# Scores of two softmax layers taken in row groups of 32 and 64 partitions, with the causal mask ahead of the score

## The chip, the cores and the metric

One core of a Trainium2 chip runs the whole program. The metric is the device time of one execution in microseconds (us). The engines are PE (TensorE, matrix products; PEld is its weight load), DVE (VectorE), ACT (ScalarE), POOL (GpSimd) and SP (SyncE, which issues most DMAs).

## What is computed

Four layers on x of 4 x 512 tokens x 128, each of the form x + attention(norm(x)) + ffn(norm(x)). The change touches the attention of layers 1 and 2:

```python
# layer 1: 16 heads of 8, each split in halves of 4: 32 causal softmax problems per batch
a1 = causal(q1, k1, v1); a2 = causal(q2, k2, v2)     # s = q k' * scale; mask; softmax; p v
y  = concat(a1 - lp * a2, a1 + lp * a2) @ Wo.T
# layer 2: 16 heads of 8, no mask
attn = softmax(Q K' / sqrt(8)); out = attn V
```

Layer 0 has windowed attention and a mixture of experts, layer 1 a second mixture of experts, layer 3 a linear attention and a dense feed-forward part.

## The kernel before

Each engine runs a fixed list of instructions. Steps of ten streams (norms, attention, feed-forward and so on) are merged into one order by the string `MERGE`: each letter takes the next step of its stream, and every engine runs its part of each step in that order. Engines meet through semaphores, and an engine that waits holds up all that stands behind on it.

For each batch b of layer 1 and 2, `stack` (L2007 to L2041, SP) stores q and k, each split in three bfloat16 parts, to DRAM and loads them back side by side, so that one bfloat16 matmul over 96 rows gives a float32 product. The rows of one head (24 in layer 1, 48 in layer 2) are spread over the 96, and those of other heads meet zeros in k. A few rows more (12 or 6) carry minus the row maximum against ones in k, which are loaded from a constant, `kone`; layer 2's k is cleared by POOL first (L1906).

Then two sweeps over the scores follow. **Maxima**: `mx` makes a unit of up to 512 columns in one of two banks of PSUM (ring `topb`), and DVE reduces it (L1485). Layer 1 has 88 such units a batch: a head's row tile sees 512, 384, 256 or 128 keys, and units of 256 or 128 are put together to 512; layer 2 has 64. **Exponentials**: `ex` makes the transposed score of one head and one key tile in one of two other banks (ring `scoreb`), with the maximum subtracted by the extra rows, and ACT takes the exponential into `pbuf` (L1820): 128 a batch in layer 1 (512, 384, 256 and 128 columns), 64 in layer 2 (512). In layer 1 a mask matmul of 128 columns over 128 rows (`identb` and `mdiagT`) is added behind each score. **Products**: `pv` multiplies four tiles of exponentials with v in float32, into four column strips of one bank, so that it uses the shape of 128 rows x 32 columns. It stands in the stream of `ex`, behind the second `ex` of the next step. `mx` of batch b+1 runs beside `ex` of batch b, with the experts of layer 1 between.

The touched lines of `mx` on PE are:

```python
m = mm(bank[:, o:o + k], HQ[lay][i][0:96, h % 8, t * P:(t + 1) * P], HK[lay][i][0:96, kof(lay, h), 0:k], True, not CAUSAL[lay])
if CAUSAL[lay]:
    m = mm(bank[:, o + k - P:o + k], mdiagT, identb, False, True)
```

Of the kernel before, what the change touches and what calls it, by code (L numbers as in the profile page):

```python
# [26 lines left out]
MERGE = (
    "11ab2ab7c2b2c2bc2bcbcbc3bcb4cb4cb3cb2cbc2b2c2bcbcj4cj2cb2c2jb2j4c3j4cbjcjc2jbjc2j2cb2cjcj2cj8c3j5cjc"
    "2j2cb2j2cj2cb2jcjc3jbc2j2bjb5j9b2cb5cbc3b3c2b3cbcb6cb2cjcjbj4cj3c2jb3c2jbcd2jcj5c2jb3j3cjb2j3c2j2cj2"
    "cb2j2cjc2jb2j3cj3cjcj2b3jb2jc2jcjcjcb4cj2c3bcbc5bcb4cb3c2b3c3b2c3bj3cb2c2jbc2jcjc2jb5jb5jb4jcb2ja4jb"  # L30
    "ja4ja2jb2j2b2jdjdjbj15bd3bdbcjbjadjba4jdjb3ja2jb4jc2jb3jd2cb2ja2jc3jba4ja7jc2j2d2eaed2ea3ea2ec79e2cd"
    "2cdc4bd5bdbd2bd7b2d3bcdbcbc6b3e2bebebeb2e2bebebe2bebebebebe3b2eb2e2bedb2e2bebe2bebebebcebe2cebe2cebe"
    "2bce2becbc3bdc2bc2e4bc2b3cb2ece2b2ebebe2becbebebcebcecec3bcdc2e2c5bcbebc2bece2bec2b2eb2cebebebecb2e2"
    "c2ebe2bebebcebebebcb2ecbc2e3c2b2ecebcbecdce2bebebebecb2e2bcebc2bc2ebcbcbcbebebd2b2e2be2bebcebebecece"
    "b2cb2c2ed2e3b2ecebce2cec2be2bebe2bebebcebe2ce2bce2cebe2bebe3c2edcbcdbc2e2cebcecbc2bdebcebc2b2c2bec2b"
    "ebce2bcebe2bebeb2ebcebecece4cbe3bdbceb2c2becbc2ecbecbceb2ecb2eb3c2e3b2ebebe3b2ecedcbecb2e2ce2c2eb2ce"
    "2becbeb2e2bec3be2bc2bcebceb2cece5bebebe3bebeb2cb2eb2cb2ce2bec2b3cbe3bec3b2e2cbcb2e3cec4b2e4bebebcbeb"
    "cbe3cbec2b2c3bcbecec5bcbcbe3b2cbebe2becb3c6bcbc4bc3bcbecbec3bcbc2be5bce5bebe4bcb2ebcbc2ecbe2bebe2b2e"
    "4be2be4b2e4be3bebe8bce2ba3b2ea5be4ba2bebe3be2be4b2e4be2bebe2be7bc5bab2e2beba2bebe3be6b2e5be4be6be2be"
    "5be9bcbebe3be7bc2bc2b2e8be3be10ba6bd2bdbd6bd4bd2bcd3bd4bc8b2ebaebebe2be2be2bebe4b2e3baebe3be4ba2e5b2"  # L40
    "e4bebe2bebe2bebebe2bebe2bebebe2bebe3bebe3bebdbe5be6bebe3bedbe2bebe2bebebe3bebed2be3b2e3bebe2bebe2beb"
    "e2bebe2bebecbebc2bebe6be2b2e8b2e3be2bebe2b2e2beb2ebdbde3bd4bed4babedbeaebe3ba2e3b2e2bedebe3bd5bebe8b"
    "ebebebebebebebe2bebebe2b2e2bebe2b2e2b2eb2e2bebebebebe2bebe2bebebcebe2bebebebebe2be2bcb2eb2e2bedebaeb"
    "eb2e2bebe2bea2e5ba2e3bebe2b2e2bebe2bebe2be2bece2be3be2b2eb2e2bebebebebe2bebe2be2b2e2b2e2b2e2bebeb2e2"
    "bebebebebe2bebe2bebebe2b2e3bebe4beb2eb2eb2e2bebe2b2e2bebebebcebe4b2ebab2e2bebece2bebebeaebecbe4be2be"
    "4baebe2b2e2bebebebebe2bebe3bebebebe2b2e2bebebebe2b2e2bebe2bebe2be2b2e2b2e2be2bc4bd2b2cbg3bf2bgcg4bf2"
    "bagbg3bg3bg2bcfba3bfbf2bg4bf3bfbgc2bf4bf3bg3bf2bg3bfg4bfbc2bc3bf4bfbc5babg5bc4bcbgbhbfc2hbfb2hahaghc"
    "ahih4c2ig2c2i4cihihcicih2cih2cich2cichchcici2cici6c")
# [107 lines left out]
def build(nc, d, out):  # L156
    ctx = ExitStack()
    with ctx:
# [122 lines left out]
        def kof(lay, h):  # L281
            return h % 8 // 4 * 4 + h // 8 if lay == 1 else h

        def tile_of(lay, n):
# [3 lines left out]
            return [(4 * n + j, 4 * n + j) for j in range(4)]

        def tops_of(lay):  # L290
            if lay == 2:
                return [((g, t, 0),) for g in range(16) for t in range(4)]
            todo = []
            for g in range(0, 32, 4):
                todo += [((g + j, t, 0),) for t in (3, 2) for j in range(4)]
                todo += [((g + j, 1, 0), (g + j + 1, 1, 2 * P)) for j in (0, 2)]
                todo.append(tuple((g + j, 0, j * P) for j in range(4)))
            return todo
# [2071 lines left out]
```

## Time and profile before

| | us |
|---|---|
| median of 3 runs (1527.28 to 1532.28) | 1531.0 |
| the profiled execution | 1529.98 |
| its span, first to last instruction | 1528.2 |
| first maxima of layer 1 alone | 588 to 676 |
| exponentials of layer 1, with maxima and experts | 676 to 1201 |
| exponentials of layer 2, with maxima | 1201 to 1447 |

The stages are read from the first and last instructions of L1485 and L1820 for each batch. A float32 matmul is recorded as two instructions. A matmul's recorded duration is its latency; what it takes of PE is the distance of its start from the next one's.

### The profile page before, as it was taken

The numbers are of one execution on the slowest core, as the hardware profiler recorded it, in microseconds if no ns is written. First come the engines' busy times: TensorE is split into PE (matmuls) and PEld (weight loads), VectorE is DVE, ScalarE is ACT, GpSimd is POOL, SyncE is SP. The second block draws the span as 40 slices with busy tenths as digits, with TensorE's granted clock in tenths as the row PEclk, the third lists the DMA queues.
The fourth block names the chain that finished last, engine by engine and source line by source line (L and its number), as shares of the span: only waits on it lengthen the run. The fifth ranks groups of instructions, "written<-read, shape, count | busy, mean of one in ns | idle before, by whom it ended". The sixth has DMA issues, their size and how long they took to land.

```text
span 1528.2 us, 23814 instructions
## 1 busy us (share of the span) xinstructions
PE 1342.3 (88%) x9318; PEld 812.0 (53%) x9334; DVE 970.2 (63%) x2093; ACT 665.5 (44%) x1424; POOL 203.0 (13%) x189
## 2 busy tenths in 40 slices
PE   7977788998897787888989989999779899999999
PEld 4455657876765674343756656654334323234565
DVE  3568743343453677876877876465667888876365
ACT  2444143753541431023433435666446566666621
POOL 1132170000202300035000000044100100000000
PEclk8988698998996987569999999999989999999988
DMA  8000123341000310015253363211212303000000
GB/s 248 6 1 1 29 67 100 98 113 49 27 1 14 70 22 3 0 41 146 89 130 109 107 168 120 92 45 29 64 20 53 64 5 66 3 1 28 1 8 21
DMA packets 65100, 86.22 MB, mean 56 GB/s; under 512 B 9566, under 2 KB 49374, under 8 KB 63326
## 3 DMA queue, kind: packets, MB, share of 16 engines
q1 hardware_dynamic: 60892, 76.30, 19.1%
q0 software_dynamic: 4096, 8.40, 2.0%
q8 instruction: 74, 1.21, 0.3%
q14 instruction: 38, 0.31, 0.1%
HBM read 62.19 MB, written 22.48 MB: 55 GB/s over the span
## 4 chain that ended last, share of the span: by engine, by line
PE 64%; DVE 14%; DMA 8%; ACT 4%; issue 4%; POOL 3%; SPq 2%; DVEq 0%; ACTq 0%
PE psA L404 32%; PE psB L404 25%; PE psB L408 5%; DVE mx L1485 3%; POOL slots_x L1922 2%; PE psA L408 2%; ACT pbuf L1738 2%; DMA wA<-slots_x 2%; POOL tH L1935 1%; DVE st L1168 1%; ACT pbuf L1820 1%; DMA arena<-scr1k 1%; DMA scr1k<-arena 1%; DMA arena<-slots_x 1%; DMA arena<-scr2k 1%
## 5 line engine op out<-in xcount | busy, mean ns | idle before, releaser
L1820 ACT ACTIVATE pbuf<-psA 128x512 f32<-128x512 f32 (+3 forms) x768 | 350.0, 489 | 250.2 <-PE psA L404 243.1
L1485 DVE TENSOR_REDUCE mx<-psA 128x1 f32<-128x512 f32 (+3 forms) x608 | 377.7, 657 | 101.2 <-PE psA L404 97.2
L404 PE MATMUL psA<-arena 64*64 64x128 f32 (+9 forms) x1632 | 243.2, 308 | 14.0 <-DVE mx L1485 11.1
L404 PEld LDWEIGHTS psA<-arena 64*64 64x64 f32 (+3 forms) x1632 | 131.5, 138 | 115.2 <-DVE mx L1485 44.2
L1738 ACT ACTIVATE pbuf<-psA,st,rq 128x128 f32<-128x128 f32 x256 | 92.7, 467 | 112.8 <-DVE st L1172 112.8
L404 PE MATMUL psA<-arena,w 96*128 96x512 bf16 (+4 forms) x320 | 114.8, 411 | 19.3 <-DMA arena<-scr2k 10.4
L404 PE MATMUL psA<-w_identb,w_mdiagT 128*128 128x128 bf16 x512 | 110.9, 243 | 0.0
L404 PE MATMUL psA<-w_mdiagT,w_identb 128*128 128x128 bf16 x512 | 110.0, 223 | 0.0
L404 PE MATMUL psB<-xf,wA 128*128 128x128 f32 x624 | 93.8, 295 | 6.1 <-DMA wA<-in_moe 5.7
L404 PE MATMUL psB<-pbuf,arena 128*5 128x512 f32 (+3 forms) x1024 | 95.3, 445 | 0.4 <-ACT pbuf L1820 0.4
L1935 POOL DMA_INDIRECT tH<-slots_y,slot_i x64 | 62.0, 968 | 237.7 <-DMA slots_y<-tH 219.3
L404 PEld LDWEIGHTS psB<-xf,wA 128*128 128x128 f32 x624 | 82.1, 204 | 13.9 <-issue 10.2
L1879 POOL TENSOR_TENSOR sm<-sm,w_ohalf 128x4 f32<-128x4 f32 x24 | 24.3, 1032 | 461.2 <-DVE sm L1045 461.0
L404 PE MATMUL psA<-w,arena 102*128 102x512 bf16 (+5 forms) x272 | 82.2, 340 | 2.2 <-ACT pbuf L1820 1.7
L1168 DVE TENSOR_REDUCE st<-psA 128x8 f32<-128x1024 f32 x32 | 39.1, 1221 | 71.0 <-PE psA L404 71.0
L1922 POOL DMA_INDIRECT slots_x<-tH,slot_i x64 | 62.1, 970 | 131.5 <-DVE slot_i L1319 74.6
L404 PEld LDWEIGHTS psA<-arena,w 96*128 96x128 bf16 (+1 forms) x320 | 38.2, 122 | 71.2 <-DVE mx L1485 27.1
L404 PE MATMUL psA<-arena,wide 128*64 128x8 f32 (+4 forms) x320 | 64.9, 301 | 11.0 <-DMA arena<-scr1k 8.1
L404 PE MATMUL psA<-arena,pbuf 128*128 128x65 f32 x512 | 70.6, 284 | 2.7 <-DVE pbuf L1192 2.6
L404 PEld LDWEIGHTS psA<-arena,pbuf 128*128 128x128 f32 x512 | 67.4, 204 | 8.8 <-issue 4.5
L404 PE MATMUL psB<-pbuf,res 128*9 128x512 f32 x512 | 66.9, 595 | 1.5 <-ACT pbuf L1820 1.4
L408 PE MATMUL psA<-w_ident,pbuf 128*128 128x128 f32 x272 | 45.3, 292 | 19.1 <-ACT pbuf L1738 10.7
(295 smaller groups left out, 2136.2 us busy)
## 6 DMA issues: line engine op xcount, KB each, us to landing
wA<-in_moe SPq DMA_DIRECT2D x39, 576.0 KB, 3.8
wA<-in_moe SPq DMA_DIRECT2D x39, 256.0 KB, 3.0
slots_x<-wA SPq DMA_DIRECT2D x20, 256.0 KB, 3.7
slots_y<-tH SPq DMA_DIRECT2D x18, 256.0 KB, 3.6
wA<-slots_x SPq DMA_DIRECT2D x15, 256.0 KB, 4.1
arena<-scr2k SPq DMA_DIRECT2D x48, 64.0 KB
scr1q<-arena SPq DMA_DIRECT2D x4, 384.0 KB, 4.0
scr1k<-arena SPq DMA_DIRECT2D x4, 384.0 KB, 4.1
```

The costliest lines, as they stand in the source:

```text
L404: return pe.matmul(out, lhsT, rhs, start=start, stop=stop, skip_group_check=True)
L408: return pe.transpose(out, in_, ident[0:n, 0:n])
L1168: dv.tensor_reduce(mx_, both("S", b, i).rearrange("p x (k c) -> p x k c", k=4), AX.X, ALU.max).then_inc(*s_max.up(b, i))
L1485: dv.tensor_reduce(m[:, t, h:h + c], topb("mx", lay, b, n)[:, 0:c * k].rearrange("p (c k) -> p c k", c=c), AX.X, ALU.max) \
L1738: a = ac.activation(sm[:, k, :], S[:, x, P * k:P * k + P], ACT.Exp, bias=st[:, 8 + 4 * x + k:9 + 4 * x + k], scale=rq(b)[:, 4 * h + k, kv, ...
L1820: ac.activation(pb(lay, b, s, j)[:, 0:T - q0_], scoreb("ex", lay, b, s, j)[:, 0:T - q0_], ACT.Exp, bias=0.0, scale=1.0) \
L1879: po.tensor_tensor(st[:, 4:8], st[:, 0:4], W["ohalf"][:, 0:4], ALU.pow).then_inc(*ln_pow.up(tag, b))
L1922: po.indirect_dma_start(Xs[lay], IndirectOffsetOnAxis(i, 0), tok[:, t * P:(t + 1) * P], None) \
L1935: po.indirect_dma_start(tH(*u)[:, t * P:(t + 1) * P], None, Ys[lay], IndirectOffsetOnAxis(i, 0)) \
```

## The change

- A head's own rows only. A score matmul now takes 24 rows (27 with the maximum) that begin at partition 0, 32, 64 or 96 in layer 1, and 48 (51) that begin at 0 or 64 in layer 2. PE is used by these in shapes of 32 x 128 and 64 x 128 instead of 128 x 128. The lists of units are reordered so that one unit and the next of a sweep use different row groups. Masks keep their 128 rows.
- The mask is written first, and the score is added to it. In `mx` one mask matmul serves all tiles of a unit: 352 in place of 512; in `ex` it stays 512.
- `stack` loads each row group by itself: 48 DMAs in place of 9 for a batch of layer 1, 24 in place of 18 in layer 2; the maxima come in 4 or 2 DMAs in place of 1. Layer 1's k takes a quarter of the bytes. `kone` is gone: POOL sets all of k to one (three memsets of 128 x 512 for layer 1 and three of 128 x 2048 in place of 128 x 4096 for layer 2).
- Buffers of k are smaller, so batch 0 of layer 2 waits for products of layer 1's batch 1 and no longer of batch 2; the ring of exponentials has 12 tiles in place of 8.
- `pv`, `tail` and the projection become an eleventh stream `k`, and `MERGE` is a new string for the whole program.

```diff
-        pb = Ring(ptiles)
+        pb = Ring(ptiles + [arena[:, 7680 + T * k:8192 + T * k] for k in range(4)])
...
+        HS = {1: 32, 2: 64}
+        HO = {1: (0, 1, 2, 3), 2: (0, 2, 1, 3)}
...
+        def q_of(lay, i, h, rows):
+            p = HS[lay] * (h // 8)
+            return HQ[lay][i][p:p + 6 * HD[lay] + rows, h % 8, :]
+
+        def k_of(lay, i, h, rows):
+            p = HS[lay] * (h // 8)
+            return HK[lay][i][p:p + 6 * HD[lay] + rows, h % 8 // 4 if lay == 1 else h % 8, :]
...
-                return [((g, t, 0),) for g in range(16) for t in range(4)]
+                return [((8 * u + g, t, 0),) for g in range(8) for t in range(4) for u in range(2)]
...
+                todo += [tuple((8 * j + g, t, o) for g, t, o in u) for u in units for j in range(4)]
...
-                i, bank = b % NBUF, topb(*u)
-                for h, t, o in tops_of(lay)[n]:
-                    k = (t + 1) * P if CAUSAL[lay] else T
-                    m = mm(bank[:, o:o + k], HQ[lay][i][0:96, h % 8, t * P:(t + 1) * P], HK[lay][i][0:96, kof(lay, h), 0:k],
-                           True, not CAUSAL[lay])
-                    if CAUSAL[lay]:
-                        m = mm(bank[:, o + k - P:o + k], mdiagT, identb, False, True)
+                i, bank, part = b % NBUF, topb(*u), tops_of(lay)[n]
+                t, c = part[0][1], len(part)
+                k = (t + 1) * P if CAUSAL[lay] else T
+                if CAUSAL[lay]:
+                    mm(bank[:, 0:c * k].rearrange("p (c k) -> p c k", c=c)[:, :, k - P:k], mdiagT,
+                       identb.unsqueeze(1).to_broadcast([P, c, P]), True, False)
+                for h, t, o in part:
+                    m = mm(bank[:, o:o + k], q_of(lay, i, h, 0)[:, t * P:(t + 1) * P], k_of(lay, i, h, 0)[:, 0:k], not CAUSAL[lay], True)
...
-                m = mm(bank[:, 0:T - q0_], HK[lay][i][0:HR[lay], kof(lay, g), kb * P:(kb + 1) * P],
-                       HQ[lay][i][0:HR[lay], g % 8, q0_:T], True, not causal)
                 if causal:
-                    m = mm(bank[:, 0:P], identb, mdiagT, False, True)
-                m.then_inc(*ex_mm.up(lay, b, s, j))
+                    mm(bank[:, 0:P], identb, mdiagT, True, False)
+                mm(bank[:, 0:T - q0_], k_of(lay, i, g, 3)[:, kb * P:(kb + 1) * P], q_of(lay, i, g, 3)[:, q0_:T], not causal, True) \
+                    .then_inc(*ex_mm.up(lay, b, s, j))
...
+                for j in range(P // HS[lay]):
+                    r, rows = HS[lay] * j, slice(HS[lay] * j, HS[lay] * j + HS[lay])
+                    for part, n in ((0, 3), (1, 2), (2, 1)):
+                        qs = dr["q"][b][part, rows].rearrange("(i g) c -> i g c", g=8)
                         for k in range(n):
...
+                            sy.dma_start(HQ[lay][i][r:r + D], qs).then_inc(*stack_in[b].up(lay))
+                            ks = dr["k"][b][k, rows].rearrange("(i g) c -> i g c", g=8)
```

**PE in layer 1**, where scores of `ex` (`psA<-w,arena`) and of `mx` (`psA<-arena,wide`) stand in a row with masks (`w_identb`, `w_mdiagT`). Before:

```order
1706 L404 MATMUL psA<-w,arena 128x256
1707 L404 MATMUL psA<-w_mdiagT,w_identb 128x128
1708 L404 MATMUL psA<-arena,wide 128x256
1709 L404 MATMUL psA<-w_identb,w_mdiagT 128x128
1710 L404 MATMUL psA<-arena,wide 128x256
1711 L404 MATMUL psA<-w_identb,w_mdiagT 128x128
```

After:

```order
1502 L412 MATMUL psA<-w_identb,w_mdiagT 128x512
1503 L412 MATMUL psA<-arena,wide 128x128 x4
1504 L412 MATMUL psA<-w_mdiagT,w_identb 128x128
1505 L412 MATMUL psA<-w,arena 128x256
1506 L412 MATMUL psA<-w_identb,w_mdiagT 128x512
1507 L412 MATMUL psA<-arena,wide 128x128 x4
```

The mask has moved ahead of its score, and one of 512 columns stands for four; between the scores of two units there is still a mask. All rows of before take 96 to 128 rows of PE; of after the masks take 128 and the scores 24 or 27.

**PE in layer 2**, where `psA<-wide,arena` and `psA<-arena,wA` are scores of `ex` and of `mx`, and `psB<-pbuf,res` is `pv`. Before:

```order
3060 L404 MATMUL psB<-pbuf,res 9x512 x4
3061 L404 MATMUL psA<-arena,wA 128x512
3062 L404 MATMUL psA<-wide,arena 128x512
3063 L404 MATMUL psA<-arena,wA 128x512
3064 L404 MATMUL psA<-wide,arena 128x512 x2
3065 L404 MATMUL psA<-arena,wA 128x512 x2
3066 L404 MATMUL psA<-wide,arena 128x512
3067 L404 MATMUL psB<-pbuf,res 9x512 x4
```

After:

```order
2764 L412 MATMUL psB<-pbuf,res 9x512 x4
2765 L412 MATMUL psA<-arena,wA 128x512
2766 L412 MATMUL psA<-wide,arena 128x512 x2
2767 L412 MATMUL psA<-arena,wA 128x512
2768 L412 MATMUL psA<-wide,arena 128x512
2769 L412 MATMUL psA<-arena,wA 128x512
2770 L412 MATMUL psA<-wide,arena 128x512 x2
2771 L412 MATMUL psA<-arena,wA 128x512 x2
2772 L412 MATMUL psB<-pbuf,res 9x512 x4
```

Scores stand side by side here as before, now with rows 0 to 50 for one and 64 to 114 for the other, and more or fewer than eight of them may stand between two `pv`.

**SP**, the loads of one batch of layer 1 behind the two stores. Before, all of them:

```order
227 L2030 DMA w<-scr1q 16x4096 x3
228 L2033 DMA arena<-scr1k 48x4096
229 L2030 DMA w<-scr1q 16x4096 x2
230 L2033 DMA arena<-scr1k 32x4096
231 L2030 DMA w<-scr1q 16x4096
232 L2033 DMA arena<-scr1k 16x4096
```

After, the first of 24 such pairs:

```order
267 L2025 DMA w<-scr1q 4x4096
268 L2029 DMA arena<-scr1k 4x2x512
269 L2025 DMA w<-scr1q 4x4096
270 L2029 DMA arena<-scr1k 4x2x512
271 L2025 DMA w<-scr1q 4x4096
```

Nine DMAs of 16 to 48 rows became 48 of 4 rows.

## Rows read from the trace of the kernel before

**Rows 1.** The page, section 1 (busy us, share) and the clock of section 2
```profile
PE 1342.3 (88%) x9318; PEld 812.0 (53%) x9334; DVE 970.2 (63%) x2093; ACT 665.5 (44%) x1424; POOL 203.0 (13%) x189
PEclk8988698998996987569999999999989999999988
```
**Rows 2.** Busy time by stretch: stretch and length, busy by engine, granted clock, DMA share, GB/s
```profile
588.00:676.00 88.00, 71.82 (x342) 34.82 (x343) 71.23 (x155) 3.78 (x8) 8.99 (x9) 0.55 0.02 7
676.00:843.00 167.00, 147.73 (x1269) 95.90 (x1268) 122.92 (x246) 68.85 (x163) 30.72 (x31) 0.94 0.44 117
843.00:1000.00 157.00, 144.00 (x1318) 102.53 (x1316) 105.71 (x215) 71.18 (x169) 0.78 (x1) 0.98 0.41 119
1000.00:1117.00 117.00, 97.01 (x827) 46.74 (x825) 66.07 (x136) 65.87 (x162) 38.84 (x36) 0.94 0.21 47
1117.00:1201.00 84.00, 79.55 (x595) 35.11 (x594) 68.54 (x138) 48.55 (x119) 4.55 (x2) 0.97 0.15 27
1201.00:1447.00 246.00, 236.08 (x1313) 88.66 (x1311) 183.44 (x371) 155.41 (x287) 4.03 (x4) 1.00 0.12 25
```
**Rows 3.** Groups by form: name, count, busy us, mean ns, idle before
```profile
L404 PE MATMUL psA<-w_identb,w_mdiagT 128*128 128x128 bf16 x512 | 110.9, 243 | 0.0
L1820 ACT ACTIVATE pbuf<-psA 128x512 f32<-128x512 f32 x384 | 213.2, 596 | 89.6 <-PE psA L404 87.3
L1485 DVE TENSOR_REDUCE mx<-psA 128x1 f32<-128x512 f32 x384 | 248.2, 685 | 63.6 <-PE psA L404 62.4
L404 PE MATMUL psA<-arena 64*64 64x128 f32 x1024 | 69.5, 291 | 0.0
```
**Rows 4.** PE in order of time, layer 1: start, us, name, rows*columns used
```profile
691.46 0.38 PE L404 MATMUL psA<-arena 108*128 108x512 bf16 x1
691.68 0.22 PE L404 MATMUL psA<-w_mdiagT,w_identb 128*128 128x128 bf16 x1
691.74 0.38 PE L404 MATMUL psA<-arena 108*128 108x512 bf16 x1
691.96 0.22 PE L404 MATMUL psA<-w_mdiagT,w_identb 128*128 128x128 bf16 x1
692.11 0.40 PE L404 MATMUL psB<-pbuf,arena 128*5 128x128 f32 x8
692.44 0.28 PE L404 MATMUL psB<-w_selq,tA 128*128 128x16 f32 x1
```
**Rows 5.** PE in order of time, layer 0: other changes of shape
```profile
51.79 1.45 PE L404 MATMUL psA<-xn,w 128*128 128x512 f32 x3
53.17 0.49 PE L404 MATMUL psA<-w_ssel,wide 64*128 64x1 f32 x3
...
288.99 0.38 PE L404 MATMUL psA<-arena,w_identb 128*128 128x512 bf16 x1
289.30 0.33 PE L404 MATMUL psA<-arena 64*64 64x128 f32 x2
```
**Rows 6.** PE in order of time, layer 2
```profile
1304.75 0.39 PE L404 MATMUL psA<-arena,wA 96*128 96x512 bf16 x1
1305.07 1.05 PE L404 MATMUL psB<-pbuf,res 128*9 128x512 f32 x8
1306.05 0.39 PE L404 MATMUL psA<-arena,wA 96*128 96x512 bf16 x1
```
**Rows 7.** SP in order of time, issuing stacks of layer 1 and layer 2
```profile
528.13 0.42 SPq L2033 DMA_DIRECT2D arena<-scr1k  x1
...
690.54 1.25 SPq L2030 DMA_DIRECT2D w<-scr1q  x3
...
1098.35 2.01 SPq L2038 DMA_DIRECT2D arena<-scr2k  x6
```
**Rows 8.** Waits of PE: for whom, us in total, times, longest
```profile
PE psA L404 <- DMA arena<-scr1k: 14.6, 2, 8.1
PE psA L404 <- DMA arena<-scr2k: 10.4, 1, 10.4
```

More of the change, by code:

```diff
@@ L25 @@
 EPS32 = float(np.finfo(np.float32).eps)
+ONE2 = float(np.array([0x3F803F80], np.uint32).view(np.float32)[0])
 MERGE = (
[L28 to L31, printed above, removed]
@@ L287, in tile_of @@
                 return [(8 * j + 4 * hf + r, 2 * j + hf) for j in range(4)]
[L288 removed]
+            return [(4 * j + n, 4 * j + n) for j in range(4)]
         def tops_of(lay):
             if lay == 2:
[L292 removed]
+                return [((8 * u + g, t, 0),) for g in range(8) for t in range(4) for u in range(2)]
             todo = []
[L294 to L297, printed above, removed]
+            for h in (0, 4):
+                units = [((h + r, t, 0),) for t in (3, 2) for r in range(4)]
+                units += [((h + r, 1, 0), (h + r + 1, 1, 2 * P)) for r in (0, 2)]
+                units.append(tuple((h + r, 0, r * P) for r in range(4)))
+                todo += [tuple((8 * j + g, t, o) for g, t, o in u) for u in units for j in range(4)]
             return todo
@@ L1901, in clr @@
             def clr(lay, b):
-                if lay == 2:
+                if lay == 1:
+                    for t in range(4):
+                        po.wait_ge(*ln_xc.at("h2", t))
+                    po.wait_ge(*bo_done.at(3))
+                    if b:
+                        po.wait_ge(*wo_mm.at(3, 1))
+                        po.wait_ge(*kn_turned.at(3, 3))
+                else:
                     po.wait_ge(*pv_mm.at(1, b + 1, 31))
-                    if b == 0:
-                        po.wait_ge(*pv_mm.at(1, 2, 31))
-                    po.memset(HK[2][b].rearrange("p g c -> p (g c)").bitcast(F32), 0.0).then_inc(*kz_done.up(b))
+                po.memset(HK[lay][b].rearrange("p g c -> p (g c)").bitcast(F32), ONE2).then_inc(*kz_done.up(lay, b))
             def rot(b, n):
@@ L2047, in mxT @@
                 sy.wait_ge(*part_m[b].at(lay))
-                sy.dma_start(HQ[lay][i][96:HR[lay], :, :], dr["m"][b].rearrange("s (j g) c -> (s j) g c", g=8)) \
-                    .then_inc(*max_in[b].up(lay))
+                for j in range(P // HS[lay]):
+                    r = HS[lay] * j + 6 * HD[lay]
+                    sy.dma_start(HQ[lay][i][r:r + 3], dr["m"][b][:, 8 * j:8 * j + 8, :]).then_inc(*max_in[b].up(lay))
             def wi3_():
@@ L2110, in streams @@
                 main += [("kn0", b, kv) for kv in range(4)] + [("v0", b, j) for j in range(4)] + [("sc", b, i) for i in range(8)]
+            take = []
             for lay in (1, 2):
@@ L2113, in streams @@
                 for b in four:
+                    main += [("ex", lay, b, s, j) for s in range(last_) for j in range(4)]
                     for s in range(last_):
-                        for j in range(4):
-                            main.append(("ex", lay, b, s, j))
-                            if j == 1 and s:
-                                main.append(("pv", lay, b, s - 1))
-                        if s and s % 4 == 0:
-                            main.append(("tail", lay, b, s // 4 - 1))
-                    main += [("pv", lay, b, last_ - 1), ("tail", lay, b, last_ // 4 - 1)]
-                    main += [("cmb1", b)] * (lay == 1) + [("pj1", lay, b), ("pj2", lay, b)]
+                        take += [("pv", lay, b, s)] + [("tail", lay, b, s // 4)] * (s % 4 == 3)
+                    take += [("cmb1", b)] * (lay == 1) + [("pj1", lay, b), ("pj2", lay, b)]
             ffn = together("h1") + [("qkv0", b, k) for b in four for k in range(3)]
@@ L2159, in streams @@
                         mix += [("yv", b, i - 1, x)] * (0 < i < 9) + [("tp", b, i, x)] * (i < 8)
-            return [norm, main, ffn, stack, top] + flows + [mix]
+            return [norm, main, ffn, stack, top] + flows + [mix, take]
         def merged():
@@ L2168, in merged @@
                 else:
-                    order += [next(todo["abcdefghij".index(c)]) for _ in range(int(n or 1))]
+                    order += [next(todo["abcdefghijk".index(c)]) for _ in range(int(n or 1))]
                     n = ""
@@ L2265, in constants @@
     c["selq1"], c["selk1"] = c["selq1"].astype(np.float32), c["selk1"].astype(np.float32)
-    one = np.zeros((3, 4, 8, T), np.float32)
-    for h in range(8):
-        one[:, h % 4, h] = 1
-    c["kone1"] = bf(one.reshape(12, 8, T))
-    one = np.zeros((3, 2, 16, T), np.float32)
-    for h in range(16):
-        one[:, h // 8, h] = 1
-    c["kone2"] = bf(one.reshape(6, 16, T))
     c["hsel"] = (i[:, None] // 8 == np.arange(16)[None]).astype(np.float32)
```

107 lines of the change are left out of this document (40 added, 67 removed).

## The prediction

> **What bounds the kernel now.** I read the busy shares first: PE is busy 88% of the span, DVE 63%, ACT 44% [rows 1]. Then the stretches by stage [rows 2], since the change works from 588 to 1447 us alone. In the layer 1 stage from 676 to 1201 us PE is busy 468.3 of 525 us (147.7 + 144.0 + 97.0 + 79.6) and DVE 363.2. In the layer 2 stage PE is busy 236.1 of 246 us, DVE 183.4, ACT 155.4. Only the first maxima, 588 to 676, have PE and DVE level (71.8 and 71.2 of 88 us), at a mean granted clock of 0.55, so mostly at the lower level of 1.2 GHz. PE is thus the bound of both stages that hold the exponentials.
>
> "Busy" counts latency, so I need what a matmul takes of PE, from the distance of starts. At full clock a score of 512 columns takes 0.22 us (691.46 to 691.68), a mask of 128 columns 0.06 (691.68 to 691.74) [rows 4]; the mean of 243 ns that a group of masks shows [rows 3] is latency. A float32 record of 512 columns takes two passes, 0.43. I went through the order of each program with these prices (by columns: 0.06, 0.11, 0.17, 0.22; 0.11 for a float32 record of 128 columns; 0.87 for a `pv` of four, which run side by side). For the layer 1 stage of before this gives 99 us of `ex` with its masks, 92 of `mx` with its masks, 69 of `pv`, 137 of experts, norms and the rest, and 26 of changes of shape (below): 423 of 525 us. For the layer 2 stage it gives 224 of 246 us, 91%.
>
> **The cost of a change of shape.** Every matmul uses PE in a shape: 128 x 128, or 128 x 32 for `pv`, 64 x 64 and a few 64 x 128 in layer 0. Where the shape changes, the next start comes late. From a mask to a `pv` it is 0.15 us instead of 0.06 (691.96 to 692.11) [rows 4]. From three float32 matmuls of 512 columns to one that takes 64 rows it is 1.38 instead of 3 x 0.43 (51.79 to 53.17), from a matmul of 512 columns to 64 x 64 it is 0.31 instead of 0.22 (288.99 to 289.30) [rows 5]. Back from `pv` to a score it is 0.98 instead of 2 x 0.43 (1305.07 to 1306.05), 0.12, of which some may be a wait [rows 6]. I take 0.095 us, both ways, for 32 x 128 too, which no row shows: its nearest row is the 64-row one, whose excess is 0.09. Between two matmuls of one shape nothing is lost.
>
> Before has 526 changes of shape, nearly all at `pv` and in layer 0. After has 2306. By stage, before to after: until the first maxima 103 to 103, first maxima 2 to 177, layer 1 stage 270 to 1769, layer 2 stage 149 to 254, rest 2 to 3. The reason is the mask. In layer 1 each of the 352 + 512 units is now a mask over 128 rows and then its scores over 24 or 27, so PE changes shape into each score group and out of it. And since a mask always stands between, no two neighbours of different row groups exist in layer 1 at all; the 160 neighbours of shape 32 x 128 are tiles of one unit, in one group.
>
> **Layer 1 stage.** (1769 - 270) x 0.095 = 142 us more of PE work, 423 to 565. Columns of scores and masks are the same; 160 fewer mask instructions save nothing, as the price goes by columns. What of the 142 is seen? Before leaves 102 us of the 525 unused by this count. Some 25 of it is waiting for DMAs (14.6 and 10.4 [rows 8]), the rest latency of loops through two banks, and clock below full (0.94, 0.98, 0.94, 0.97 [rows 2]). With PE slower, exponentials and maxima are ready when PE asks, and part of those gaps goes. I take the share that layer 2's stage reaches now, 91%: 565 / 0.91 = 621, or **+96 us**. Bounds: nothing absorbed, +142; only the 25 us of DMA waits and 6 more left, 596, +71. DVE (363 us) stays far below.
>
> **First maxima.** They have 175 changes more. The units of four heads are 11, with 5120 columns of scores and 2048 of masks: 3.0 us at full clock, and twice that, 6.0, at the lower one, which rules here. 22 changes add 2.1 us to such a group, and at most twice that if they double with the clock: 8.1 to 10.2. The stretch has 88 us for eight such groups and the norms, 11 each, of which DVE is busy 8.9. So PE goes from below DVE to level with it: 0 to +17 us, and I take **+6**, nearer to the low end since DVE's time hides most of it.
>
> **Layer 2 stage.** 105 changes more cost 10 us. Against it, neighbours from different row groups may run side by side. The trace has no row for shape 64 x 128 at two places; the nearest is 64 x 64, whose two matmuls start within one latency of 0.33 us [rows 5] and whose 1024 take 69.5 us busy instead of 1024 x 0.291 = 298 one behind the other [rows 3]. Taken from the order, 199 disjoint pairs of different groups stand side by side in layer 2: at best 199 x 0.22 = 43 us. But in 193 of them the second waits for a bank, and a bank comes back once per 0.685 us from DVE and 0.596 from ACT [rows 3]. So the second of a pair mostly starts late anyway. A third of the 43, 14, less 10 gives **-4**; bounds -33 and +10.
>
> **DMAs, buffers, order.** SP takes 0.42 us for a load of 16 rows (1.25 for three), 0.335 for one of 8 (2.01 for six) [rows 7]. A batch of layer 1 has 48 in place of 9. At 0.27 (the two rows drawn on to 4 rows) to 0.335 this is 13 to 16 us of SP in place of 4. Batch 0's last load left SP at 528 us [rows 7], 60 before the first maxima, so its ten more us are hidden; batch 1's first maxima now come after 53 `ex` where they came after 24. Behind the loads on SP are loads of expert weights, with two or three blocks in hand; PE could wait there once or twice: +3, bounds 0 and +15. Three POOL memsets more stand where POOL idles. Layer 2's first stack no longer waits for batch 2's products and its maxima begin earlier in the order, against a wait of 10.4 [rows 8]: -3, bounds -10 and 0. `pv` as own stream, with 12 tiles: it lets `ex` run ahead, which only fills gaps that I have already given away.
>
> **Sum.** 96 + 6 - 4 + 3 - 3 = +98 on the profiled execution's 1530.0, which is 1 below the median: 1628.
>
> **Rivals.**
>
> *Faster.* Changes to the narrow shapes cost nothing and the pairs run together. For it: the 64 x 64 pairs [rows 3]. Against it: both shapes of 64 rows lose 0.09 on entry [rows 5]. Price: layer 2 -20 to -43, transition -5, so 1530 - 35 = 1495. It decides if the excess per change is under 0.02 us.
>
> The Trainium skill, page "TensorE: Matmul & The Clock Gate", section "Part 3: Packing small matmuls", gives 3.07x for four 32-row matmuls of 512 columns in four row groups; by it layer 1's scores would gain most. The order shows none such side by side in layer 1. The page "TensorEngine Tiling (Array Packing)", section "Key Properties", says that a change of tiling mode drains the engine; it names no time.
>
> *Hidden.* Most changes fall where PE waits for a bank anyway, since a mask's wait and the change run together. For it: 102 unused us. Against: PE idles 57 us in the stage (525 - 468), 25 of them for DMAs, so some 32 are waits for ACT or DVE [rows 2, 8]. It gives about +45: 1575.
>
> *Clock.* With PE streaming about 400 of some 620 us in layer 1, the clock falls to 1.2 GHz in places, as it does from 588 to 676 us (0.55 [rows 2]). Streaming work at half clock for a tenth of it adds 40, and changes grow: 1680.
>
> **How the numbers follow.** Likeliest (1600 to 1660): 0.60. Hidden (1550 to 1600): 0.17. Clock (over 1660): 0.16. Faster rival: 0.05, the remaining 0.02 within 0.3% or little above. A measurement of this kernel can tell 0.3%, 5 us, from no change. The range leaves out the faster rival, the deepest hiding and the far end of the clock: 1570 to 1690. Faster 0.05, same 0.02, slower 0.93.
>
> **What would show it.** After, in layer 1: mask to score 0.15 us, score of 512 to mask 0.31. PE nearly without idle from 676 on, that stage about 620 us, DVE and ACT with more idle time ahead of the maxima and the exponentials, ended by PE. In layer 2: starts of two scores within 0.01 us of each other where both banks are free, the stage near 242 us. Wrong if a score starts 0.06 behind its mask, if the stage of layer 1 shows PE waiting much longer for DMAs, or if the clock row shows new stretches of 5.

## The result, and the profile after

| | before | after |
|---|---|---|
| median of the runs taken together with those of after, us | 1529.1 | 1881.2 (1853.8 to 1896.8) |
| profiled execution, us | 1530.0 | 1880.7 |
| its span, us | 1528.2 | 1878.9 |
| mean granted clock over the span | 0.899 | 0.750 |

The changed kernel takes 1.221 times the time of the kernel before, 95% interval 1.205 to 1.237: 351 us more in the profiled execution, where the prediction had 98. The ratio is taken over runs within 1.5% of the fastest of their kernel, here 1853.8 and 1880.7 us of after; its other two took 1881.7 and 1896.8. The direction was right, the size and the range were not. The page of the changed kernel, sections 1 and 2, against [rows 1]:

```profile
PE 1713.1 (91%) x9174; PEld 874.9 (47%) x9174; DVE 988.2 (53%) x2093; ACT 679.0 (36%) x1422; POOL 199.8 (11%) x192
PEclk8887899899797555555688768855655557999989
```

DVE and ACT do nearly what they did. PE is busy 371 us more, and from the 14th slice to the 33rd its clock is mostly at 5 or 6. Before, the layer 1 stage (slices 18 to 31) stood mostly at 9. The prediction had named new stretches of 5 as a sign that it would be wrong. Busy time by stretch, before and then after; the columns are those of [rows 2]:

```profile
588.00:676.00 88.00, 71.82 (x342) 34.82 (x343) 71.23 (x155) 3.78 (x8) 8.99 (x9) 0.55 0.02 7
676.00:1201.00 525.00, 468.30 (x4004) 280.29 (x4003) 363.23 (x732) 254.45 (x611) 74.89 (x69) 0.96 0.33 88
1201.00:1447.00 246.00, 236.08 (x1313) 88.66 (x1311) 183.44 (x371) 155.41 (x287) 4.03 (x4) 1.00 0.12 25
1447.00:1528.00 81.00, 76.51 (x319) 46.59 (x314) 44.80 (x111) 17.40 (x32) 1.01 (x1) 0.85 0.04 14
```
```profile
587.00:674.00 87.00, 84.25 (x267) 30.95 (x266) 67.38 (x126) 1.73 (x4) 1.26 (x1) 0.50 0.01 3
674.00:1559.00 885.00, 841.36 (x3944) 368.26 (x3943) 401.59 (x827) 272.17 (x614) 74.75 (x75) 0.63 0.18 50
1559.00:1807.00 248.00, 232.96 (x1299) 83.77 (x1297) 177.94 (x371) 156.56 (x291) 5.83 (x5) 0.92 0.13 25
1807.00:1879.00 72.00, 66.54 (x332) 39.61 (x330) 44.13 (x113) 16.64 (x31) 1.01 (x1) 0.98 0.04 15
```

The layer 1 stage takes 885 us in place of 525, at a granted clock of 0.63 in place of 0.96. The other stretches change by -1, -1, +2 and -9; -1 - 1 + 360 + 2 - 9 = 351. So the whole loss stands in one stage. PE in order of time in that stage, at the 2.4 GHz level and then at the 1.2 GHz level, against [rows 4]:

```profile
1001.43 0.23 PE L412 MATMUL psA<-w_identb,w_mdiagT 128*128 128x128 bf16 x1
1001.59 0.39 PE L412 MATMUL psA<-arena,wide 24*128 24x512 bf16 x1
1001.91 0.23 PE L412 MATMUL psA<-w_identb,w_mdiagT 128*128 128x128 bf16 x1
1002.07 0.38 PE L412 MATMUL psA<-arena,wide 24*128 24x512 bf16 x1
...
1400.18 0.60 PE L412 MATMUL psA<-arena 27*128 27x512 bf16 x1
1400.71 0.29 PE L412 MATMUL psA<-w_mdiagT,w_identb 128*128 128x128 bf16 x1
1400.93 0.60 PE L412 MATMUL psA<-arena 27*128 27x512 bf16 x1
```

Mask to score is 0.16 us and score of 512 columns to mask 0.32 at full clock (0.15 and 0.31 were forecast), so a change of shape costs about 0.10 us. At the lower level they are 0.22 and 0.53: the columns take twice the time, 0.107 and 0.427, and the change still 0.10 to 0.11. Over all changes between a mask and a score the median excess is 0.103 to 0.111 us, by kind and level. The changes cost nearly what I said. What I did not say is that most of the stage would run at the lower level: a mean of 0.63 is about three quarters of the time at 0.5.

A count as in the prediction splits the stage; it is an estimate, as it takes one mean clock for the whole stage. PE's columns are 397 us of work at full clock (423 less the 26 of changes). At the clocks shown they take 397 / 0.96 = 414 before and 397 / 0.63 = 630 after: +216. Changes take 26 before and 1769 x 0.108 = 191 after: +165. What is left was 85 and is 64: -21. Together 360.

### The profile page after: what moved, and what is told of

Same layout as the page of the kernel before. It is cut to its first block, busy times and chain, and to the rows that moved or that the text cites. A ratio compares the mean times of both kernels' runs of the same rounds, so it can differ in the third digit from the quotient of the medians.

```text
span 1878.9 us, 23694 instructions
## 1 busy us (share of the span) xinstructions
PE 1713.1 (91%) x9174; PEld 874.9 (47%) x9174; DVE 988.2 (53%) x2093; ACT 679.0 (36%) x1422; POOL 199.8 (11%) x192
## 3 DMA queue, kind: packets, MB, share of 16 engines
q0 software_dynamic: 4096, 8.40, 1.5%
## 4 chain that ended last, share of the span: by engine, by line
PE 76%; DVE 8%; SPq 5%; DMA 4%; ACT 4%; issue 2%; DVEq 0%; ACTq 0%
PE psA L412 42%; PE psB L412 27%; PE psB L416 5%; SPq L2029 2%; SPq L2025 2%; ACT pbuf L1747 2%; PE psA L416 2%; DVE st L1177 1%; DMA wA<-slots_x 1%; DMA arena<-scr2k 1%; DVE mx L1494 1%; ACT pbuf L1829 1%; DMA scr1k<-arena 1%; DMA arena<-scr1k 0%; DVE arena L1096 0%
## 5 line engine op out<-in xcount | busy, mean ns | idle before, releaser
L1829 ACT ACTIVATE pbuf<-psA 128x512 f32<-128x512 f32 (+3 forms) x512 | 242.6, 489 | 379.4 <-PE psA L412 376.8
L412 PE MATMUL psA<-arena 64*64 64x128 f32 (+9 forms) x1632 | 281.9, 327 | 0.0
L1829 ACT ACTIVATE arena<-psA 128x512 f32<-128x512 f32 (+3 forms) x256 | 121.5, 491 | 147.5 <-PE psA L412 146.7
L412 PE MATMUL psA<-arena,w 48*128 48x512 bf16 (+5 forms) x320 | 135.8, 506 | 16.9 <-DMA arena<-scr2k 12.7
L412 PEld LDWEIGHTS psA<-w_mdiagT,w_identb 128*128 128x128 bf16 x512 | 55.2, 108 | 177.8 <-issue 102.6
L412 PE MATMUL psA<-w_identb,w_mdiagT 128*128 128x128 bf16 (+2 forms) x352 | 108.2, 307 | 31.9 <-DMA arena<-scr1k 31.2
L412 PEld LDWEIGHTS psA<-w_identb,w_mdiagT 128*128 128x128 bf16 x352 | 37.5, 106 | 126.9 <-issue 47.1
L412 PE MATMUL psA<-w,arena 51*128 51x512 bf16 (+5 forms) x272 | 83.1, 379 | 2.8 <-ACT pbuf L1829 1.4
L412 PE MATMUL psA<-wide,arena 51*128 51x512 bf16 (+4 forms) x192 | 72.8, 399 | 2.8 <-ACT pbuf L1829 1.4
L412 PE MATMUL psA<-arena,wide 128*64 128x8 f32 (+5 forms) x320 | 73.0, 339 | 1.2 <-DVE sq L1140 0.7
```

What stands on the lines that cost most here:

```text
L412: return pe.matmul(out, lhsT, rhs, start=start, stop=stop, skip_group_check=True)
L1829: ac.activation(pb(lay, b, s, j)[:, 0:T - q0_], scoreb("ex", lay, b, s, j)[:, 0:T - q0_], ACT.Exp, bias=0.0, scale=1.0) \
```

## Experiments

Three theories. **A**: changes of shape cost their 0.1 us, and the empty time at them takes the clock down. **B**: matmuls over few rows take the clock down. **C**: the rest of the change (order, loads, `pv` as own stream) costs a large part. Where no interval is given, a kernel ran once. Beside the first four of these the kernel before ran seven times: six took 1526.7 to 1533.1 us, one 1947.1.

**Full rows.** The changed kernel with its scores over all rows:

```diff
-            return HQ[lay][i][p:p + 6 * HD[lay] + rows, h % 8, :]
+            return HQ[lay][i][0:P, h % 8, :]
...
-                ac.activation(pb(lay, b, s, j)[:, 0:T - q0_], scoreb("ex", lay, b, s, j)[:, 0:T - q0_], ACT.Exp, bias=0.0, scale=1.0) \
+                ac.activation(pb(lay, b, s, j)[:, 0:T - q0_], scoreb("ex", lay, b, s, j)[:, 0:T - q0_], ACT.Exp, bias=0.0, scale=0.0) \
```

`k_of` is changed like `q_of`, and q's buffers are cleared first.

> The kernel after, with every score matmul over all 128 rows of the stacks (so over all heads of the stack at once: the scores are not the reference's, and the exponential is taken of zero times them). The order, the mask ahead of the score, the product stream, the DMAs and the columns of every matmul stay. q's buffers are set to zero first, six memsets more on POOL. Changes of shape fall from 2306 to 526. Theory A (the changes of shape cost their 0.1 us each and take the clock down): 1500 to 1550 us, clock near 0.9 as before. Theory B (the few rows of the scores take the clock down): the same, 1500 to 1550. Theory C (the new order, the DMAs of 4 rows and the product stream cost a large part): 1600 or more. So this run tells C from A and B.

Measured: 1552.5 us median, 1.0146 of the kernel before (1.0118 to 1.0174). The layer 1 stage and the layer 2 stage:

```profile
651.00:1232.00 581.00, 469.29 (x3902) 280.85 (x3952) 383.92 (x827) 254.54 (x615) 80.04 (x78) 0.91 0.28 76
1232.00:1470.00 238.00, 226.52 (x1262) 87.73 (x1285) 178.74 (x370) 156.88 (x290) 7.57 (x6) 1.00 0.13 26
```

The time is just above the forecast of 1500 to 1550. C is worth about 22 us; the scores in row groups hold the rest. Yet the order and the loads do move time about: the layer 1 stage is 56 us longer than before and the first maxima 21 shorter. Of the 56, 52 are longer waits for stacks and weights (83.1 us in place of 30.7 in that stage). PE's waits over the whole span, with full rows:

```profile
PE psA L412 <- DMA arena<-scr1k: 51.6, 3, 24.1
PE psA L412 <- DMA arena<-scr2k: 21.6, 1, 21.6
```

Against 14.6 and 10.4 [rows 8]. In the changed kernel itself they are 31.2 and 12.7: PE is slower there, so it waits less for loads.

**No masks.** The changed kernel without the masks of layer 1, so that only rows are few and 1048 changes are left:

> The kernel after without any mask in layer 1, so layer 1's attention is not causal. Scores keep their 24 to 51 rows and their row groups; changes of shape go down by well over a thousand, and in layer 1 neighbours of different groups now stand side by side. Streaming work falls by 55 us. Theory A (changes cause the loss, by their time and through the clock): the clock returns to 0.85 or more and the time to 1450 to 1550. Theory B (few active rows take the clock down, whatever stands between): the clock stays near 0.75 and the time at 1650 to 1750.

The edit takes out the `mm` of the mask in `mx` and in `ex`. Measured: 1622.3 us, mean clock 0.81, between the two forecasts. The layer 1 stage is 652 to 1302, with 682 changes left in it:

```profile
652.00:1302.00 650.00, 536.90 (x3170) 243.76 (x3172) 386.60 (x826) 253.33 (x614) 75.20 (x75) 0.73 0.24 68
```

It has fewer instructions than the kernel with full rows, waits less for its loads (37.4, 18.0 and 16.0 us against 46.7, 21.6 and 14.8), and takes 69 us more. Neither theory alone gives that.

**Narrow masks.** The kernel before, scores over their 96 and 108 rows, masks over 32:

```diff
-                        m = mm(bank[:, o + k - P:o + k], mdiagT, identb, False, True)
+                        m = mm(bank[:, o + k - P:o + k], mdiagT[0:32], identb[0:32], False, True)
```

The mask in `ex` is changed the same way.

> The kernel before, its order and its scores over 96 to 108 rows, with one edit: the mask matmuls of layer 1 take 32 rows of their operands instead of 128 (a quarter of the mask is applied). That puts two changes of shape around each of 1024 masks and leaves the scores wide. Theory A: 2048 x 0.1 = 205 us of changes and a clock near 0.75: 1800 to 1950. Theory B: the changes' own time alone, 1650 to 1720, clock 0.85 or more. If changes cost nothing: 1530.

Measured: 1796.6 us, mean clock 0.82, with 2461 changes by the order (1935 more than before). The layer 1 stage takes 773 us:

```profile
698.00:1471.00 773.00, 747.45 (x4004) 347.91 (x4004) 375.17 (x730) 268.74 (x610) 75.70 (x69) 0.77 0.23 60
```

Changes with wide scores (and masks of few rows) cost 265 us or 0.137 each: more than the bare 0.1, since the clock falls too. Again the clock lies between the two forecasts.

**Layer 2 alone.** The kernel before with the row groups in layer 2 only (`HS`, `stack`, `q_of` and `k_of` as in the change, order of before).

> The kernel before with one part of the change: layer 2's scores in row groups of 64, neighbours from different groups, k set to one by POOL. Layer 1, the mask, the products and the order stay. Computes the reference. 49 to 105 more changes of shape in layer 2 (5 to 10 us), against two scores side by side where both banks are free. Theory: the waits for banks leave little to pairs, layer 2's stage stays within 10 us of 246, 1520 to 1535 us. Rival (pairs work, DVE becomes the bound): 1490 to 1510.

Measured: 1.0201 of the kernel before (1.0148 to 1.0253), so +31 us, against both forecasts. The four runs took 1556.6, 1565.2, 1587.2 and 2951.9 us, and the ratio rests on the first two alone. The forecast had counted the changes wrong as well: the trace holds 755 in place of 526, so 229 more and not 49 to 105, 117 of them in the stretch just ahead of the layer 2 stage and 107 in it. At 0.1 us each that is 23 of the 31 us, an estimate.

**Test row of matmuls.** The kernel before with a row of matmuls behind its last PE step:

```diff
+                def one(k, rows, at, cols=T):
+                    mm(banks[k % 4 if rows == P else at // 32][:, 0:cols], identb[at:at + rows], four[at:at + rows, 0:cols // P] if cols > P else identb[at:at + rows, 0:cols],
+                       True, True)
...
```

> The kernel before, unchanged, with a row of test matmuls behind its last PE step, all bfloat16, constants as data. Between stretches of 300 matmuls of 128 rows x 512 columns (about 64 us at the 2.4 GHz level) stand in this order: 300 of 32 rows in one row group; 600 of 32 rows, neighbours in four groups and banks; 300 of 64 rows in one group; 600 of 64 rows, neighbours in two groups; 200 pairs of 128 rows x 128 columns and 32 rows x 512 columns (400 changes of shape); the same 200 pairs with 128 rows each (no change); 1500 of 128 rows x 32 columns; 200 groups of three 128-row matmuls of 512 columns and one 32-row one of 128 columns (400 changes). Theory A (a change of shape costs its 0.1 us and the empty time at changes is what takes the clock down): granted clock 1.00 in every stretch without changes, 32 rows among them, 0.5 to 0.7 in the 200 changing pairs, 0.9 or more in the groups of four, and 300 narrow matmuls take 64 us. Theory B (few active rows take the clock down): 32 rows in one group run at 0.5 to 0.6 and take 120 us, 64 rows at up to 0.8, four groups side by side at 1.00, and the changing pairs no lower than the 32 rows alone. Both: four groups side by side take 35 to 50 us for 600, if side by side works as in layer 2.

Its stretches: 128 rows; 32 rows in one group; four groups by turns; 64 rows in one group; two groups by turns; the 200 changing pairs; the same pairs with 128 rows; groups of three wide and one narrow.

```profile
1525.00:1588.00 63.00, 63.00 (x294) 28.55 (x293) 0.00 (x0) 0.00 (x0) 0.00 (x0) 1.00 0.01 5
1596.00:1711.00 115.00, 115.00 (x271) 38.20 (x269) 0.00 (x0) 0.00 (x0) 0.00 (x0) 0.50 0.00 0
1780.00:1811.00 31.00, 31.00 (x580) 14.64 (x576) 0.00 (x0) 0.00 (x0) 0.00 (x0) 1.00 0.01 3
1877.00:1941.00 64.00, 64.00 (x298) 27.88 (x297) 0.00 (x0) 0.00 (x0) 0.00 (x0) 1.00 0.00 1
2007.00:2070.00 63.00, 63.00 (x586) 28.40 (x584) 0.00 (x0) 0.00 (x0) 0.00 (x0) 1.00 0.00 1
2141.00:2284.00 143.00, 143.00 (x381) 38.00 (x380) 0.00 (x0) 0.00 (x0) 0.00 (x0) 0.50 0.00 0
2351.00:2403.00 52.00, 52.00 (x385) 29.41 (x383) 0.00 (x0) 0.00 (x0) 0.00 (x0) 1.00 0.00 1
2578.00:2757.00 179.00, 179.00 (x788) 59.27 (x788) 0.00 (x0) 0.00 (x0) 0.00 (x0) 1.00 0.00 1
```

Matmuls of 32 rows, one behind the other without a gap, run at 0.50: 0.42 us each (115 / 271). A held that narrow rows alone keep the clock, and it falls. B holds for 32 rows, but its forecast of up to 0.8 for 64 rows came out as 1.00. PE was busy for all of the 32-row stretch and its shape never changed. Four groups by turns keep 1.00 and take 0.054 us each, a quarter of 0.216. Two groups of 64 take 0.108 each. The pairs of 128 and 32 rows run at 0.50 and take 0.74 us each (200 in 147.7 us), 640 columns at the lower level (0.53) and two changes of 0.10.

The Trainium skill, page "TensorE: Matmul & The Clock Gate", section "Part 1: The HAM clock gate", says that the clock follows how busy PE has been. Here PE was busy all the time and the clock stood at the lower level; what differs from the stretch at 1.00 before it is the rows in use, 32 for 128, and with them the shape. The Trainium skill, same page, section "Part 3: Packing small matmuls", gives 3.07x for four matmuls in four row groups. This test row shows 0.216 / 0.054 = 4.0x against one matmul of 512 columns at the same clock.

**Second test row.** To part rows from changes. The seven stretches stand in the order of the expectation: pairs with 64 rows; pairs with a strip of 32 columns; 32 rows in two groups by turns; one wide and four side by side; pairs with 96 rows; 128 rows x 512 with 32 rows x 128; four wide and one narrow.

> The kernel before with a second row of test matmuls at its end, bfloat16, constants as data, 300 of 128 rows x 512 columns between the stretches: 200 pairs of 128 rows x 128 columns and 64 rows x 512 (400 changes); 200 pairs of 128 x 128 and 128 rows x 512 into a strip of 32 columns (400 changes, all rows active); 600 of 32 rows in two groups by turns; 150 times one of 128 rows x 512 columns and four of 32 rows x 512 in four groups (300 changes); 200 pairs of 128 x 128 and 96 rows x 512, of one shape; 200 pairs of 128 rows x 512 and 32 rows x 128 (400 changes, as in the narrow-mask kernel); 200 times four of 128 rows x 512 and one of 32 rows x 512 (400 changes). Theory A (empty time at changes): every stretch with 200 pairs and changes at 0.5 to 0.7, the 96-row pairs and the two groups at 1.00. Theory B (active rows): the strips and the 128 rows x 512 with 32 x 128 at 1.00, the 64-row pairs at 1.00 (64 rows alone were), the two groups at 1.00. If the two add up, so that the chip sees rows and time together: the 64-row pairs at 0.5, strips and narrow masks at 0.5 to 1.00, four wide and one narrow at 1.00. One wide with four side by side: 0.21 + 0.21 + 0.2 = 0.63 us each at 1.00 in both.

```profile
1597.00:1741.00 144.00, 144.00 (x380) 39.23 (x379) 0.00 (x0) 0.00 (x0) 0.00 (x0) 0.50 0.00 0
1809.00:1904.00 95.00, 95.00 (x395) 37.02 (x395) 0.00 (x0) 0.00 (x0) 0.00 (x0) 1.00 0.00 1
1970.00:2034.00 64.00, 64.00 (x595) 28.77 (x596) 0.00 (x0) 0.00 (x0) 0.00 (x0) 1.00 0.00 1
2101.00:2196.00 95.00, 95.00 (x731) 28.76 (x730) 0.00 (x0) 0.00 (x0) 0.00 (x0) 1.00 0.00 1
2262.00:2316.00 54.00, 54.00 (x392) 30.45 (x390) 0.00 (x0) 0.00 (x0) 0.00 (x0) 1.00 0.00 1
2383.00:2477.00 94.00, 94.00 (x393) 36.64 (x392) 0.00 (x0) 0.00 (x0) 0.00 (x0) 1.00 0.00 1
2545.00:2799.00 254.00, 254.00 (x988) 78.95 (x988) 0.00 (x0) 0.00 (x0) 0.00 (x0) 1.00 0.00 0
```

Rows and changes act together, as the third forecast had it. 64 rows without a change keep 1.00, and strips of 32 columns with all rows and 400 changes keep 1.00 (0.48 us a pair, of which 0.2 empty); but 64 rows together with the changes run at 0.50. So A's 0.5 to 0.7 for every stretch of changing pairs and B's 1.00 for the 64-row pairs are both wrong. The third stretch parts rows from shape: in the same shape of 32 x 128, without a change, one group in use runs at 0.50 and two by turns at 1.00. The sixth is the pattern of the narrow masks, and there it keeps 1.00, where the kernel with narrow masks fell to 0.77; that kernel also has scores of fewer columns and other waits, and which of these takes its clock down was not tested. One wide matmul and four side by side in four groups take 97 us for 150, 0.65 each, at 1.00: such an order, with masks together, was not built for the kernel.

**Rows of 64 in the changed kernel.** The edit is that of "full rows" with 64 rows in place of all; 2236 changes are left.

> The changed kernel, with each layer 1 score over 64 rows (0 to 63 or 64 to 127) in place of 24 or 27, and each of layer 2 over 64 in place of 48 or 51; q is cleared and the exponential is taken with scale 0, so the softmax is left out and the times are those of the same instructions. Columns, order, masks and DMAs stay, and 2236 changes of shape of 2306. Theory A (the empty time at the changes takes the clock down, rows don't matter): 1840 to 1900 us, mean clock 0.75, the layer 1 stage 850 or more. Theory B (few active rows take it down, as they did in the test row, where 32 rows alone ran at 0.50 and 64 at 1.00): 1680 or less, clock 0.85 or more, the stage 650 to 700. If both act, between: about the 1795 us and 0.82 of the kernel of before with narrow masks.

Measured: 1720.7 us, mean clock 0.85, between B's forecast and that for both together. The layer 1 stage and the layer 2 stage:

```profile
679.00:1406.00 727.00, 663.53 (x3939) 315.54 (x3938) 395.44 (x824) 266.52 (x613) 80.41 (x78) 0.83 0.22 61
1406.00:1646.00 240.00, 224.89 (x1296) 81.96 (x1295) 178.14 (x370) 156.46 (x290) 7.57 (x6) 0.96 0.13 26
```

This is the cut that divides the loss. Order, columns and (but for 70) changes are those of the changed kernel, and 160 us are gone. On PE the number of active rows is touched, with it the shape of layer 1's scores (64 x 128), and the values: k is set to ones and the exponentials are ones. In the test rows, where all operands come from one identity matrix, the rows alone do the same; a run of this kernel with other values was not made. By profiled spans: before 1528, order and loads 1542 (+14), scores of 64 rows with their changes of shape 1719 (+177), 24 to 51 rows in place of 64 1879 (+160). The sum is 351. The +177 is not the price of changes alone: 1710 changes more at 0.105 us are 180 us by themselves (an estimate), the clock of the layer 1 stage falls from 0.91 to 0.83, and its waits for stacks and weights shrink from 83 to 59 us. Each step rests on one profiled run, and the four runs of the changed kernel lie 43 us apart.

**Masks in the row group.** The changed kernel with each mask as four matmuls of 32 rows, all in the score's group (shown for `ex`; `mx` likewise):

```diff
-                    mm(bank[:, 0:P], identb, mdiagT, True, False)
+                    g0 = 32 * (g // 8)
+                    for x in range(4):
+                        mm(bank[:, 0:P], W["ident4"][g0:g0 + 32, x, :], W["mdiag4"][g0:g0 + 32, x, :], x == 0, False)
```

> The changed kernel, with every mask written as four matmuls of 32 rows in the row group of its score, from constants laid out for it; all that is computed stays. Changes of shape fall from 2306 to 1048, which by the measured 0.108 us takes 136 us away; mask columns in layer 1 count four times, 52 us of PE becoming 207 at the 2.4 GHz level. Theory A (changes take the clock down): mean clock 0.87 or more, and the layer 1 stage about 397 + 155 + 60 = 610 to 700 us, so 1610 to 1700 in all. Theory B (few active rows take it down): clock 0.65 to 0.75 and all of it at about half clock, so the stage 950 to 1150 us and 1950 to 2150 in all.

Measured: 1858.9 us, mean clock 0.76. The layer 1 stage:

```profile
686.00:1532.00 846.00, 785.58 (x6265) 444.72 (x6263) 398.16 (x825) 260.63 (x613) 75.78 (x75) 0.65 0.19 53
```

The clock is close to B's 0.65 to 0.75, although 1258 changes are gone; A's 0.87 is far off. The time is below B's forecast of 1950 to 2150, which had all of the stage near half clock, where it was 0.65: (397 + 155) / 0.65 = 849 us, an estimate that leaves no room for the 681 changes still in the stage, so part of the work seems to have run side by side. How much was not measured.

**Maxima without masks.** Theirs can be left out of the maxima sweep for good: a larger maximum is subtracted from all scores of a row and drops out of the softmax (so long as the hidden scores of a row are not so far above the seen ones that the exponentials vanish; the data here are not like that). First in the changed kernel:

> The changed kernel, with no mask in the maxima sweep of layer 1: 352 mask matmuls and 551 changes of shape fewer (1755 left of 2306); the softmax is unchanged by a larger maximum that is subtracted. Neighbouring score units of the maxima then stand in different row groups without a mask between. Theory A: the measured 351 us over 1780 added changes is 0.197 us for each, clock included; 551 fewer give 109 us and 29 us of masks at a mean clock of 0.63 another 46: 1881 - 155 = 1726, clock 0.79. Theory B: only the masks and the bare 0.1 us go: 1881 - 46 - 59 = 1776, clock 0.75 still.

Measured: 1754.1 us, mean clock 0.78, midway between 1726 and 1776; it does not tell the two apart, as both act. Then in the kernel before:

```diff
-                           True, not CAUSAL[lay])
-                    if CAUSAL[lay]:
-                        m = mm(bank[:, o + k - P:o + k], mdiagT, identb, False, True)
+                           True, True)
```

> The kernel before, with no mask in the maxima sweep of layer 1 (512 fewer mask matmuls of 128 columns, 29 us of PE by the 0.057 us that one takes). The maximum then runs over keys that the mask would hide too; it is subtracted before the exponential and drops out of the softmax, so nothing that is computed is left out. Changes of shape stay 526. Theory A and theory C alike: PE is the bound in the layer 1 stage, its other waits stay, so 10 to 29 us less: 1500 to 1520. If the two-bank loop with DVE rather than PE bounds the maxima: 1528, no change. Theory B expects the same as A.

Measured: 1513.2 us, 0.9896 of the kernel before (0.9861 to 0.9931). That is 16 us less than the kernel before, within the forecast of 1500 to 1520. Its layer 1 stage:

```profile
668.00:1182.00 514.00, 451.43 (x3618) 258.09 (x3617) 360.26 (x728) 252.59 (x609) 75.17 (x68) 0.94 0.34 89
```

That is 11 us of the 22 that 384 masks take there by 0.057; the first maxima give 8 more.

**Layer 2 again, and with 64 rows.** Beside this pair the kernel before took 1643.6 us, so the two are compared with each other only.

> The kernel with layer 2 alone in row groups of 64, a second profiled execution beside the next kernel. If its loss of 2% is one of the row groups, the layer 2 stage takes 265 us or more where the kernel of before takes 246, at a granted clock of 0.93 or less. If it stands elsewhere (SP's six loads in place of nine, POOL's memsets, the first maxima), the stage takes 240 to 250 us and the time is missing before it.

> The same kernel, with each layer 2 score over 64 rows (0 to 63 or 64 to 127) in place of 48 or 51; shape, changes of shape and order are the same. q is cleared first and the exponentials of layer 2 are taken with scale 0, so its softmax is left out. Theory rows (active rows, and not the shape in which PE is used, take the clock down): the stage of layer 2 at 0.95 or more and within 8 us of 246, and 15 to 25 us less in all than the same kernel with 48 and 51 rows. Theory changes (only the changes of shape do): no difference between the two above 5 us.

Measured: 1687.6 and 1669.4 us. The layer 2 stage of the first and of the second:

```profile
1329.00:1603.00 274.00, 250.97 (x1314) 87.15 (x1313) 183.86 (x373) 156.09 (x287) 4.03 (x4) 0.88 0.13 22
```
```profile
1328.00:1588.00 260.00, 236.58 (x1313) 83.10 (x1311) 183.29 (x373) 155.82 (x287) 4.03 (x4) 0.94 0.13 24
```

Every other stretch agrees between the two within 4 us, and the layer 2 stage takes 14 us less when 64 rows are active in place of 48 and 51, in the same shape and order. That fits the rows in use. It does not show it: the first of the two kernels had 285 us and a clock of 0.83 for this stage in its earlier profile, 11 us from the 274 here. The forecast's 0.95 and its 8 us around 246 were missed (0.94 and 260).

## Why the prediction went wrong

- **Bound.** Right. PE bounds the stages, before and after (841 of 885 us busy in layer 1); DVE and ACT do the same work and only wait longer.
- **Cost of a change of shape.** 0.095 us was taken for shapes that no row showed, and 0.103 to 0.111 was measured for 32 x 128, at either level of the clock. For 1769 changes that is 23 us more than the prediction had.
- **What is absorbed.** I let 46 of the 142 us be hidden in gaps; by the count above 21 were. The term should have stood near its upper bound.
- **The clock: the step that failed.** The sum kept the clock of before for the layer 1 stage. The rival *Clock* had the mechanism in part (empty time) and priced it for "a tenth" of the streaming work, +40. The clock fell to 0.63 over the whole stage, +216. I had read 0.55 in the first maxima [rows 2] as the price of idle PE, and took the narrow shapes to be free of such an effect, though no row showed a long stretch of them. 32 active rows stood at the lower level with PE fully busy (0.50), and 64 rows did so once changes stood between them (1.00 without, 0.50 with). The range ended at 1690 since the rival was given too short a stretch; by the stage's columns, all of it at the lower level would have been 565 + 397 = 962 us, and the measured 885 lies between.
- **First maxima.** +6 forecast, -1 measured. The order alone takes 21 away (67 us with full rows, clock 0.91), and the row groups give 20 back (87 us, clock 0.50). With 64 rows it is 87 us at 0.50 as well, so here 64 rows give nothing back. Why the clock there is 0.55 before and 0.91 with full rows was not settled.
- **Layer 2.** -4 forecast, +2 measured, and that from two parts: -8 from the order (238 with full rows) and +10 from the row groups, my upper bound. Pairs do start together, as [rows 5] had suggested:

```profile
1663.60 0.39 PE L412 MATMUL psA<-arena,wA 48*128 48x512 bf16 x1
1663.61 0.39 PE L412 MATMUL psA<-wide,arena 51*128 51x512 bf16 x1
1664.20 0.39 PE L412 MATMUL psA<-arena,wA 48*128 48x512 bf16 x1 [0.21 <-DVE mx L1494]
```

  The bank that the next one waits for comes back from DVE 0.6 us later, as said. The gain is eaten by changes and by the clock (0.92 for 1.00). In the order of before the same edit loses 31 us. It has 229 changes more there, against 101 in the layer 2 stage here (247 for 146); but its stage was 274 and 285 us in two profiles with 253 or 254 changes, where the changed kernel's takes 248 with 247, and why is open.
- **DMAs.** +3 forecast within 0 to 15. PE waits for stack and weight DMAs 41.4 us in the stage (28.7 and 12.7) in place of 30.7 (14.6, 10.4 and 5.7): +11. With full rows 83 us are waited there (46.7, 21.6 and 14.8), and with 64 rows 59 (41.2, 12.8 and 5.3): the faster PE is, the more it waits for loads. What SP takes was mis-sized. I had 0.27 to 0.335 us for a load of 4 rows, 13 to 16 us a batch; it took 0.46 for q and 0.61 for k, and batch 0's loads held SP for 28 us, from 556.6 to 584.6, where before they took 4. The last one left SP 2 us ahead of the first maxima and not 60:

```profile
583.50 0.46 SPq L2025 DMA_DIRECT2D arena<-scr1q  x1
584.00 0.61 SPq L2029 DMA_DIRECT2D arena<-scr1k  x1
```

- **Earlier stack of layer 2.** -3 forecast; the wait went from 10.4 to 12.7.
- **After layer 2.** Not in the sum, -9: the last stretch runs at 0.98 in place of 0.85. It does so with full rows too, so it comes from the order.

## What to carry to other kernels

Before a matmul is made narrower, ask what fills the other rows of PE at the same time: if nothing does, the columns cost the same at one clock and the clock may halve (0.216 us with 128 rows, 0.42 with 32). Keep neighbours of one shape together and put what has another shape (a mask, a bias) into long rows of its own, since each change costs 0.1 us both ways, and with few rows in use the clock falls as well. Price a fall of the clock for the whole stage that has the new pattern, not for a part of it.
